# Attention openings of a four-block transformer kernel: projections and values ahead of the score chunks, the first group's parts read back in quarters

## The reference

```python
# first attention: rotary turn of the first 8 of 16 channels of each head, no mask
q, k, v = (proj(wq), proj(wk), proj(wv))        # x normalised, 16 heads of 16 channels
q, k = apply_rope(q, k, sin, cos)
att = softmax(einsum('bhqd,bhkd->bhqk', q, k) / sqrt(16))
y = einsum('bhqk,bhkd->bhqd', att, v)
x = x + y @ wo.T
...
# second attention: causal mask and a bias linear in the distance
attn = einsum('bhqd,bhkd->bhqk', q, k) / sqrt(16) + alibi_bias + causal_mask
x = x + einsum('bhqk,bhkd->bhqd', softmax(attn), v) @ W_o
```

## Time and profile before

| | us |
|---|---|
| median of 3 runs (lowest, highest) | 3001.02 (2999.36, 3005.0) |
| the profiled execution, its own time | 3007.55 |
| its span, first to last instruction | 3005.8 |
| PE busy | 2670.5 (89%) |
| DVE busy | 1951.0 (65%) |
| ACT busy | 1263.7 (42%) |
| first attention, first PE instruction to first unit | 230.2 to 337.8 |
| first attention, units, to about | 1095 |
| second attention, first PE instruction to first unit | 1862.8 to 1942.0 |
| second attention, units, to about | 2553 |

### The profile page before, as it was taken

How to read it: one execution, slowest core, us unless ns; L and a number is a source line. 1 busy time by engine, 2 the same in 40 slices (tenths; PEclk the granted TensorE clock), 3 DMA queues, 4 the chain that set the end, 5 groups by cost and what they waited for, 6 DMA issues and landing times. The chain is left out here.

```text
span 3005.8 us, 40300 instructions
## 1 busy us (share of the span) xinstructions
PE 2670.5 (89%) x14292; PEld 1280.2 (43%) x14292; DVE 1951.0 (65%) x4227; ACT 1263.7 (42%) x1901; POOL 657.4 (22%) x640
## 2 busy tenths in 40 slices
PE   3985899999999999797999994699999999799997
PEld 2442233333333332354455662344444544455554
DVE  5875887887877886485774334567667674576333
ACT  1431355655655657543211221155555556221321
POOL 0540331231321400153002431212111100000342
PEclk8997799999999999998999997799999999899998
DMA  3003321303303200001202653633233330300566
GB/s 115 1 1 79 64 43 28 59 20 51 59 17 48 51 15 1 1 1 64 87 32 49 142 125 85 108 57 62 45 65 65 60 54 2 105 32 26 119 140 165
DMA packets 161155, 175.78 MB, mean 58 GB/s; under 512 B 19186, under 2 KB 132786, under 8 KB 160818
## 3 DMA queue, kind: packets, MB, share of 16 engines
q1 hardware_dynamic: 144388, 151.26, 22.8%
q0 software_dynamic: 12416, 17.84, 3.6%
q10 hardware_dynamic: 4160, 4.19, 0.4%
HBM read 116.32 MB, written 56.13 MB: 57 GB/s over the span
## 5 line engine op out<-in xcount | busy, mean ns | idle before, releaser
L1744 DVE TENSOR_REDUCE a_mx<-a_bank 128x1 f32<-128x512 f32 (+3 forms) x1792 | 1032.4, 628 | 327.7 <-PE a_bank L1494 249.9
L1626 ACT ACTIVATE a_E<-a_bank 128x1024 f32<-128x1024 f32 (+3 forms) x896 | 795.8, 932 | 430.5 <-PE a_bank L1549 298.4
L1494 PE MATMUL a_bank<-a_KT,a_QT 96*128 96x512 bf16 (+4 forms) x1792 | 582.2, 371 | 89.2 <-DMA a_KT<-parts 50.5
L1549 PE MATMUL a_bank<-a_QT,a_KT 99*128 99x512 bf16 (+4 forms) x1792 | 511.7, 361 | 12.9 <-DMA a_QT<-a_mT 10.5
L1564 PE MATMUL a_bank<-a_E,a_Vg 128*32 128x512 f32 (+3 forms) x3584 | 442.0, 565 | 0.7 <-ACT a_E L1626 0.7
L1494 PEld LDWEIGHTS a_bank<-a_KT,a_QT 96*128 96x128 bf16 (+1 forms) x1792 | 151.0, 98 | 571.3 <-DVE a_mx L1744 295.6
L1549 PEld LDWEIGHTS a_bank<-a_QT,a_KT 99*128 99x128 bf16 (+1 forms) x1792 | 171.2, 99 | 190.6 <-ACT a_E L1626 34.3
L848 PE MATMUL d_bank<-wdT,d_hT 128*128 128x256 f32 (+1 forms) x768 | 202.6, 408 | 22.2 <-DVE x L1054 22.2
L960 ACT ACTIVATE d_silu<-d_bank 128x512 f32<-128x512 f32 x96 | 57.2, 596 | 380.8 <-PE d_bank L835 377.1
L1044 DVE SCALAR_TENSOR_TENSOR d_silu<-d_silu,d_bank 128x512 f32<-128x512 f32 x96 | 65.6, 683 | 232.3 <-ACT d_silu L960 232.2
L433 POOL TENSOR_TENSOR f_hl<-f_hT,f_hh 128x512 f16<-128x512 f32 x96 | 111.1, 1157 | 392.1 <-ACT f_hh L452 392.1
(11 more groups left out here) (224 smaller groups left out, 3624.3 us busy)
## 6 DMA issues: line engine op xcount, KB each, us to landing
parts<-a_parts SPq DMA_DIRECT2D x64, 384.0 KB, 2.5
a_QT<-parts SPq DMA_DIRECT2D x192, 128.0 KB, 5.4
a_KT<-parts SPq DMA_DIRECT2D x192, 128.0 KB, 8.4
d_wgu<-in_L_ffn_w_gate SPq DMA_DIRECT2D x64, 176.0 KB
d_wgu<-in_L_ffn_w_up SPq DMA_DIRECT2D x64, 176.0 KB
d_wd<-in_L_ffn_w_down SPq DMA_DIRECT2D x64, 176.0 KB
normalised<-d_xn SPq DMA_DIRECT2D x8, 1152.0 KB, 4.7
acc<-d_zero SPq DMA_DIRECT2D x66, 128.0 KB, 1.8
```

The costliest lines, as they stand in the source:

```text
L1494: last = nc.tensor.matmul(out[:, 0:w], QT[0:W, h, qt * P:(qt + 1) * P], KT[0:W, h, kh * HALF:kh * HALF + w], start=True, stop=not diag)
L1549: last = nc.tensor.matmul(out, KT[:, h, kt * P:(kt + 1) * P], QT[:, h, half * HALF + c0:(half + 1) * HALF], start=True, stop=not diag)
L1626: nc.scalar.activation(E[:, u % 2, 2 * pair:2 * pair + 2, c0:HALF], bank[:, 2 * pair:2 * pair + 2, c0:HALF], ACT.Exp).then_inc(exps, 1)
L1744: nc.vector.tensor_reduce(mx[:, j, qt, kh:kh + 1], out[:, 0:w], AX.X, ALU.max).then_inc(freed_dve, 1)
```

## The change

It does five things, all in `attention_phase`.

- `opening` becomes: four tokens, all eight projections, four values (`ahead_of_rows`), then chunks only.
- Banks: items of `ahead_of_rows` use banks 0 to 4 in turn (the unit banks, not yet in use), all later ones banks 5 to 7 as before. `earlier[x]` is the last item that used x's bank; the first unit waits for the last eviction of `ahead_of_rows`.
- Keys are projected ahead of queries: items 0 and 1 of a batch are the key halves, 2 and 3 the query halves of the first eight heads.
- Group 0 of batch 0 is read back by `load_first(eng, n)` in quarters of six DMAs of 64 KB, each when its own write has landed: quarter 1 is issued from ACT, the others from SP. The chunk list has the query half as its outermost loop, and PE waits for quarters 0 to 2 before chunk 0, for quarter 3 (`loaded_last`) before the first chunk of the second query half.
- The stages of projections 4 to 7 of the first batch lie in `y` and `E` instead of `Z` and `R`, so all four are evicted without waiting for POOL; their shuffles (first attention) stand ahead of the chunks on DVE.

```diff
-              for j in range(GH) for qt in range(TPB) for kh in range(2)
+              for h in range(QH) for j in range(GH) for qt in range(h * KPH, (h + 1) * KPH) for kh in range(2)
...
-    opening = ([("tokens", 0, n) for n in range(4)] + [("proj", 0, n) for n in range(4)]
-               + some(0, 4) + [("value", 0, 0)] + some(4, 8) + [("value", 0, 1)] + some(8, 12) + [("value", 0, 2)]
-               + some(12, 16) + [("value", 0, 3)] + some(16, 20) + [("proj", 0, 4)] + some(20, 27) + [("proj", 0, 5)]
-               + some(27, 34) + [("proj", 0, 6)] + some(34, 41) + [("proj", 0, 7)] + some(41, C + 3)
-               + [("turn_m", 0)] + some(C + 3, C + AHEAD))
+    ahead_of_rows = ([("tokens", 0, n) for n in range(4)] + [("proj", 0, n) for n in range(NJ)]
+                     + [("value", 0, n) for n in range(4)])
+    opening = ahead_of_rows + some(0, C + 3) + [("turn_m", 0)] + some(C + 3, C + AHEAD)
...
+        own = n % 5 if n < len(ahead_of_rows) else 5 + (n - len(ahead_of_rows)) % SB
+        banks[x], earlier[x], holder[own] = own, holder.get(own), x
...
         def staged(b, n):
-            return (E[:, 0, n, :], E[:, 1, n, :]) if b == 0 and n < 4 else (Z[:, n % 2, :], R[:])
+            if b == 0 and n >= 4:
+                return y[:, 2 * (n - 4):2 * (n - 3), :].rearrange("p a d -> p (a d)"), E[:, 1, n - 4, :]
+            return (E[:, 0, n, :], E[:, 1, n, :]) if b == 0 else (Z[:, n % 2, :], R[:])
...
+        def load_first(eng, n):
+            eng.wait_ge(written[n], START + 16)
+            dst, q, which = ((KT, 1, (1, 0, 2, 1, 0, 0)) if n < 2 else (QT, 0, (0, 0, 0, 1, 1, 2)))
+            at_ = slice(n % 2 * HALF, (n % 2 + 1) * HALF)
+            for s in range(6):
+                eng.dma_start(dst[s * HD:(s + 1) * HD, 0:GH, at_],
+                              dram["parts"][0, q, which[s], 0:GH * HD, at_].rearrange("(j d) t -> d j t", d=HD)
+                              ).then_inc(loaded_last if n == 3 else loaded[0], 16)
...
-                for n in range(4):
-                    write(0, n)
-                load(0, 0)
+                write(0, 0)
+                write(0, 1)
+                load_first(sp, 0)
+                write(0, 2)
+                write(0, 3)
+                load_first(sp, 2)
+                load_first(sp, 3)
                 load(0, 1)
...
                         if x[1] % C == 0:
-                            pe.wait_ge(loaded[G % NG], START + (b + 1) * 12 * 16)
+                            pe.wait_ge(loaded[G % NG], START + ((b + 1) * 12 + (6 if G % NG == 0 else 0)) * 16)
+                        if G == 0 and qt == KPH and j == kh == 0:
+                            pe.wait_ge(loaded_last, START + 6 * 16)
...
-                for x in opening:
+                for x in ahead_of_rows[0:8]:
                     take(x)
-                    if x == ("proj", 0, 3):
-                        cast(0)
-                        for n in range(4):
-                            if n < 3:
-                                cast(n + 1)
-                            cast_rest(n)
+                rest_of = ahead_of_rows[8:]
+                cast(0)
+                for n in range(4):
+                    if n < 3:
+                        cast(n + 1)
+                    cast_rest(n)
+                    if not second:
+                        take(rest_of[n])
+                load_first(act, 1)
+                for x in rest_of[0 if second else 4:]:
+                    take(x)
```

39 lines of the change are left out of this document (25 added, 14 removed).

## The result

The changed kernel takes **2953.14 us** (median of 4 runs, 2950.72 to 2956.61) against 3001.97 us for the kernel before (4 runs, 2999.36 to 3005.0): ratio 0.9832, 95% interval 0.9814 to 0.985. Measured again later (run e11_change_again) it is 2948.64 us against 3002.99, ratio 0.9829 (0.9811 to 0.9848). The gain is 49 to 51 us where 43 were forecast, so the direction and the mechanism held and 6 to 8 us are to be explained.

What follows compares the result with a forecast made beforehand. PE was taken to bound the units, so an earlier first unit ends each attention earlier. Savings of 25.7 and 17.3 us, together 43.0, took the profiled 3007.6 to 2964.6, less 6.5 to the median: 2958.0 us, range 2951 to 2974.

Steps and rivals of the forecast that it cites:

- part 1: Openings: values and projections moved into PE's read-back wait let chunks run at DVE's pace, saving 18.1 and 11.2 us.
- a sign of being wrong: Second opening: PE waiting for ACT's evictions was listed as showing the forecast wrong.
- the bound of 2.9 us: Second opening: if the clock falls while PE stands for ACT, its last three values end 2.9 us late; 0 was taken.
- part 2: Read-back in quarters: chunk 0 starts 5.9 us earlier in the first attention and 4.4 us earlier in the second.
- The first rival: Read-back: the quarters come hardly sooner, the DMA engines being full; 2965.4 us, or 2968.3 with no gain; chance 0.14.
- transfer sum: First opening: transfers rather than issues, all at 155 GB/s, put chunk 0 at 267.1, 3.7 us later.
- part 3: From `maxima` to the first unit: 1.7 us saved in each attention.
- Rivals 2 and 3: DVE bounds the second attention's units, 2973.8 us, chance 0.07; PE stays at 1.2 GHz into the units, 3043.5, chance 0.02.
- part 4: Units of both attentions: same instructions, so a gain of 0.
- The correction to the median of the runs (6.5 us): Whole program: the profiled execution lies 6.5 us above the median of the runs, so 2964.6 became 2958.0.

Runs made afterwards that it cites:

- e11_change_again: The changed kernel itself measured once more, nothing changed: 2948.64 us against 3002.99 for the kernel before, ratio 0.9829.
- e5: The changed kernel with quarter 1 issued on SP's queue, between write 3 and quarter 2, instead of on ACT's: 2955.35 us, ratio 0.9846.
- e8: The changed kernel with twenty unused additions put on GpSimd's queue around the first attention's first maxima: 2952.96 us (one run).
- e2: The kernel before with the new order of chunks and nothing else: 3000.52 us, ratio 0.9993.
- e12: The kernel before with VectorE's statistics and aggregation at the inner batch boundaries taken apart, old chunk order kept: 2994.22 us, ratio 0.9971.
- e9: The changed kernel with VectorE's statistics and aggregation at the three inner batch boundaries taken apart: 2944.67 us, ratio 0.982.

## Why the prediction was right, and where it was off

**PE's long wait as cover (part 1): right.** Projections and values ahead of the chunks cost nothing, and PE still waited behind them. The wait is 7.6 us instead of about 5, because back to back a projection takes 14.49 / 8 = 1.81 us and a value 1.77, not the 1.98 and 1.99 of the earlier trace rows. The stream of reduces is 38.40 us, as forecast. One piece of the reasoning was incomplete: the text put all of DVE's idle time down to PE's work between the chunks, but PE itself also waited 3.9 us there for evictions that stood behind POOL, which the change's stages removed.

**Second opening (part 1): right within a microsecond or so.** PE's stand for ACT, which the text both forecast and listed as a sign of being wrong, was there (1.86 us), cost nothing, and the three values behind it ended 1.29 us ahead of chunk 0 (1.4 forecast). The clock did fall in that stand, as the bound of 2.9 us supposed, but for the first value only:

```profile
1851.77:1858.90 7.13, 7.13 (x24) 5.65 (x24) 0.00 (x0) 3.10 (x6) 6.30 (x8) 0.76 0.69 193
```

The first of the three took 3.6 us and the other two 2.0 and 1.9. The stream of reduces was 23.44 us instead of 24.3, which nearly makes up for the two terms that came out smaller (chunk 0 earlier by 3.9 us for 4.4, `maxima` to first unit shorter by 1.1 for 1.7): 17.1 us in all for 17.3.

**Quarters (part 2): right, by two misses that cancel.** 6.5 and 3.9 us for chunk 0 in the first pair of profiles, forecast 5.9 and 4.4; 6.7 and 4.9 by taking them out. In the first opening write 2 took 3.5 us to land instead of 3.0 and SP issued quarter 0 in 3.25 us instead of 2.68, so quarter 2 was issued 0.8 us later than forecast, counted from PE's first instruction; chunk 0 then came 1.7 us behind its last issue, where the text took 3.1 and at least 2.4. The first rival, whose transfer sum gave 3.7 us less in the first opening, is refuted: chunk 0 came 32.7 us behind PE's first instruction, below even the forecast's 33.2 (263.4 - 230.16). The rule of the Trainium skill, DMA: Bandwidth & Descriptors, section Issuing engines are not separate DMA queues, held in its plain sense: in e5 the second queue's worth was 1.2 us of issue time ahead of quarter 2, and 1.4 us of the opening. The transfer sum that the prediction drew from it did not come out in this opening.

**Maxima to first unit (part 3): right in the first attention**, 9.7 us for 11.4, and e8 shows that GpSimd's operations slow the small ones. In the second it was 7.98 us for 9.05, where about 7.3 were forecast.

**Rivals 2 and 3: refuted.** Units 2 did not grow by 15.8 us in any profile with the new order. The clock was back soon: 4.5 us behind the first unit a pair of score products still takes 1.04 us, at 5.5 us 0.59:

```profile
315.14 1.04 PE L1574 MATMUL a_bank<-a_QT,a_KT 99*128 99x512 bf16 x2
316.23 0.59 PE L1574 MATMUL a_bank<-a_QT,a_KT 99*128 99x512 bf16 x2
```

**What was mis-sized: the openings before the change, and part 4.**

First, the sum took the stream of 56.47 us and the start of chunk 0 (39.2 us behind PE's first instruction) from one profiled execution. The same opening ran in two more kernels (e2, whose order makes no difference among the equally wide chunks of the first attention, and e12): 111.12 and 111.17 us, not 107.66. In e2 and e12 the first projection that PE does between reduces at half speed comes one earlier. e2:

```profile
288.59 1.98 PE L1517 MATMUL a_bank<-a_xT,wqkvT 128*128 128x512 f32 x4 [0.20 <-DVE a_mx L1744]
293.96 3.61 PE L1517 MATMUL a_bank<-a_xT,wqkvT 128*128 128x512 f32 x4 [0.21 <-DVE a_mx L1744]
301.58 3.22 PE L1517 MATMUL a_bank<-a_xT,wqkvT 128*128 128x512 f32 x4
```

In the profile of before the second of them still took 1.98 us, at 292.03. The stream is 2.6 and 2.8 us longer in e2 and e12 than in before; another 0.9 and 0.7 us lie ahead of chunk 0. The mean of the three openings is 110.0 us; that of the same opening behind the change (after, e11, e9) is 81.5: 28.5 us instead of 25.7. For the second opening, by before and e12 against after, e11, e8 and e9, it is 79.8 - 60.7 = 19.1 instead of 17.3.

Second, "The units: 0" in part 4 left out the batch boundaries. The new order of chunks makes PE's stall there 1.70 instead of 1.96 us, and the clock doesn't always fall: 2.3 us on average, by the estimate above.

Together 28.5 + 19.1 + 2.3 = 49.9 us, against 49 to 51 measured. This sum was made afterwards, from means of two to four profiles each, so it shows where the missing us can lie and no more. The two profiled executions themselves differ by 3007.55 - 2950.72 = 56.8 us: 26.2 + 17.1 + 5.7 lie in the three stretches, and 7.5 in the stretch between the two attentions, from the end of the first attention's last product with the values to PE's first instruction of the second. No part of the change touches it; it took 640.4 us in the profile of before and 632.6 to 639.7 in all others. The correction to the median of the runs (6.5 us) left such differences out; that the profile was high in that stretch and low in opening 1 at once, the prediction couldn't know.

## What to carry to other kernels

Before you ask for more banks or buffers, look whether the work between the steps of the bounding stream can go into a wait that is there anyway: here the order, with the stages that it needs, gave most of 31 us, the banks 1 to 3. Where work on the path runs at either level of TensorE's clock, its duration in one profile is one draw; price it at both levels, or read the same stretch in several executions, since taking such work off the path also takes away the draw. And look for single long blocks on the engine that feeds the bound: 2 us of statistics in one piece, met at each batch boundary, cost some 9 us in this kernel (6 to 12 by the interval). But look where the pieces go: in the second attention, with reduces between them, no wait above 0.6 us was left, while in the first the last piece came right ahead of another block and PE waited 2.94 us.

## What the runs showed of the hardware

- The same stall of 1.70 us of TensorE is followed by a fall of the granted clock in some executions and not in others (15 of 27), a stall of 1.96 us was followed by one each time (6 of 6). One fall costs 1.7 us.
- Chunks of 512 columns at 1.2 GHz keep VectorE's reduces without a gap: 38.36 us busy of 38.40.
- A small operation of VectorE on SBUF that starts while GpSimd is in one ends within 0.05 us of its end: 0.47 instead of 0.18 us beside additions of 0.61 to 0.66 us, up to 1.02 beside ones of 1.19. Of those that started as GpSimd's was just ending or starting, three took their usual 0.18 or 0.19 us.
- Six DMAs of 64 KB took 2.7 to 3.8 us to issue on SP's queue, and 3.3 to 3.7 on ACT's in the first opening, 2.7 to 2.9 in the second.
